# Preparing attention: PE's untaken path as one loop over the halves, five small loads later, the first shift split at once

## The reference

```python
def _L0_attn_ref(x, Wq_d, bq_d, W_qk, b_qk, Wkv_d, bkv_d, Wv_u, bv_u, Wo, bo):   # 32 heads, latent of 4
    C_q = x @ Wq_d + bq_d                                   # (b, s, 12)
    C_kv = x @ Wkv_d + bkv_d                                # (b, s, 4): keys, the same for all heads
    q = (C_q @ W_qk + b_qk).reshape(b, s, NUM_HEADS, KV_LAT)
    scores = jnp.einsum('bqhd,bkd->bhqk', q, C_kv) / jnp.sqrt(jnp.asarray(KV_LAT, x.dtype))
    attn = jax.nn.softmax(scores, axis=-1)
    V = (C_kv @ Wv_u + bv_u).reshape(b, s, NUM_HEADS, HEAD_DIM)
    out = jnp.einsum('bhqk,bkhd->bqhd', attn, V).reshape(b, s, NUM_HEADS * HEAD_DIM)
    return out @ Wo + bo
...
x = x + _L0_attn_ref(_layernorm(x), ...)
x = x + _L0_ffn_ref(_layernorm(x), ...)                     # x @ W.T + bias + sum over 8 LoRA pairs of rank 16
```

## Time and profile before

| | us |
|---|---|
| three runs | 2072.43, 2073.54, 2073.84; median 2073.54 |
| profiled execution | 2071.58 |
| its span | 2069.7 |
| ACT busy, L636 of it | 1968.8, 1900.0 |
| PE busy | 1959.6 |
| DVE, POOL busy | 468.2, 207.3 |

### The profile page before, as it was taken

One profiled execution on the slowest core, in us unless ns is written; L12 is line 12 of the kernel. 1 busy time (PEld: TensorE's weight loads), 2 busy tenths in 40 slices (PEclk: granted clock), 3 DMA queues, 4 the chain that ended last, 5 costly groups with the idle time before them and its releaser, 6 DMA issues.

```text
span 2069.7 us, 36111 instructions
## 1 busy us (share of the span) xinstructions
PE 1959.6 (95%) x15134; PEld 718.4 (35%) x15134; DVE 468.2 (23%) x1134; ACT 1968.8 (95%) x2185; POOL 207.3 (10%) x212
## 2 busy tenths in 40 slices
PE   8878898999999999999999999999999999999999
PEld 5522222333333333333333333333333333333337
DVE  7613433111121210211121111211111111212115
ACT  6699999999999999999999999999999999999980
POOL 5500010000110002000110001100100001100022
PEclk9999999999999999999999999999999999999999
DMA  8532010000010001000010000100010000100011
GB/s 323 149 124 86 3 48 3 5 25 26 13 36 16 18 21 46 5 13 26 26 36 3 26 25 20 30 15 26 15 45 5 25 14 26 36 16 13 25 42 41
DMA packets 45806, 77.43 MB, mean 37 GB/s; under 512 B 15886, under 2 KB 29766, under 8 KB 45642
## 3 DMA queue, kind: packets, MB, share of 16 engines
q1 hardware_dynamic: 43296, 75.02, 10.7%
q10 hardware_dynamic: 2346, 0.09, 0.1%
HBM read 51.23 MB, written 23.86 MB: 36 GB/s over the span
## 4 chain that ended last, share of the span: by engine, by line
ACT 43%; PE 36%; issue 17%; DVE 0%; DVEq 0%
ACT probs L636 43%; PE ps L941 17%; PE ps L986 10%; PE ps L930 6%; PE ps L975 2%; PE ps L964 0%; PE ps L970 0%; PE ps L666 0%; DVE y L1463 0%; PE ps L1083 0%; PE ps L1079 0%; DVE o_t L1519 0%; ACT o_t L651 0%; ACT o_sb L648 0%; DVE recip L1511 0%
## 5 line engine op out<-in xcount | busy, mean ns | idle before, releaser
L636 ACT ACTIVATE probs<-ps 128x1024 f32<-128x1024 f32 x2048 | 1900.0, 1029 | 19.5 <-PE ps L930 8.9
L941 PE MATMUL ps<-probs,c_wide 128*32 128x512 f32 x8192 | 985.2, 598 | 0.0
L930 PE MATMUL ps<-q_in,key_t 27*128 27x512 bf16 x4096 | 404.5, 385 | 97.6 <-ACT probs L636 90.9
L986 PE MATMUL ps<-w_eff,xn_t 128*128 128x512 f32 x1344 | 394.4, 418 | 0.0
L941 PEld LDWEIGHTS ps<-probs,c_wide 128*32 128x32 f32 x8192 | 212.3, 108 | 424.5 <-issue 219.3
L930 PEld LDWEIGHTS ps<-q_in,key_t 27*128 27x128 bf16 x4096 | 103.0, 91 | 726.5 <-ACT probs L636 715.0
L1463 DVE SCALAR_TENSOR_TENSOR y<-ps,nw,y 128x512 f32<-128x512 f32 x64 | 48.1, 751 | 979.4 <-PE ps L986 967.9
L986 PEld LDWEIGHTS ps<-w_eff,xn_t 128*128 128x128 f32 x1344 | 228.1, 188 | 101.9 <-issue 69.8
L536 POOL TENSOR_TENSOR y<-y,ffn_bias 128x1024 f32<-128x1024 f32 x32 | 76.4, 2388 | 1349.0 <-DVEq L1484 1349.0
L531 POOL TENSOR_TENSOR y<-y,attn_bias 128x1024 f32<-128x1024 f32 x32 | 75.8, 2384 | 467.0 <-DMA y<-in_L_attn_x_dram 466.9
L1447 DVE TENSOR_TENSOR y<-ps,y 128x512 f32<-128x512 f32 x56 | 38.7, 692 | 135.4 <-PE ps L964 135.4
(11 more groups left out here) (170 smaller groups left out, 607.0 us busy)
## 6 DMA issues: line engine op xcount, KB each, us to landing
y<-in_L_attn_x_dram SPq DMA_DIRECT2D x40, 512.0 KB, 4.3
out_dram<-y SPq DMA_DIRECT2D x31, 512.0 KB, 2.7
area<-in_L_attn_x_dram SPq DMA_DIRECT2D x16, 512.0 KB, 9.0
q_in<-q_parts SPq DMA_DIRECT2D x256, 27.0 KB
q_parts<-q_parts_sb SPq DMA_DIRECT2D x48, 128.0 KB, 3.0
xn<-in_L_attn_x_dram SPq DMA_DIRECT2D x8, 512.0 KB, 9.1
y<-in_L_attn_Wo_dram SPq DMA_DIRECT2D x1, 2048.0 KB, 8.5
xn<-in_L_attn_Wo_dram SPq DMA_DIRECT2D x1, 2048.0 KB, 13.4
```

The lines of the kernel that those rows point to most:

```text
L636: nc.scalar.activation(probs[:, (c * STEPS + step) % PROBS, bass.ts(pair, 2 * N)], ps[:, 2 * (i % SCORE_SLOTS):2 * (i % SCORE_SLOTS) + 2, ...
L930: last = nc.tensor.matmul(ps[:, at, :], key_t[TILE * h:TILE * h + KEYS, bass.ts(b * KT + kt, P)], q_in[TILE * h:TILE * h + KEYS, g % 2, :] ...
L941: last = nc.tensor.matmul(ps[32 * h:32 * h + 32, SUMS, :], c_wide[:, b * KT + kt, at:at + 32], probs[:, (c * STEPS + step) % PROBS, bass.t ...
L986: last = nc.tensor.matmul(ps[:, SHARED, :], xn_t[:, t % 2, a, kb, :], w_eff[:, b, kb, bass.ts(half, N)], start=(kb + i == 0), stop=(kb == ...
```

## The change

Three edits:

1. In PE's general path the two copies of the loop over chunks, one for each half, become one loop over the halves around one loop over chunks. Since a matmul inside a loop can't choose the half's keys by the loop's variable here, ACT first copies the half's keys and weights into `key_half` and `bound_half`, and PE waits for them (`m_keys`). All of it lies in the path that is jumped over when `tight` is 1.
2. SP's five small loads go from behind `load_tiles(RING + 3)`, ahead of the query stores of chunks 2 to 5, to behind `store_shifts(0, 1, CB)`, ahead of Wv.
3. On DVE the first half's `split_shift` runs through without a break; `scale_parts(7)` and then `split_latents(6)` follow. Before, `split_latents(6)` and `scale_parts(7)` stood between its second and third part.

```diff
@@ sync
             load_tiles(RING + 3)
-            sp.dma_start(bv_rows, ...).then_inc(lora_in, 16)
-            sp.dma_start(coef, ...).then_inc(lora_in, 16)
-            sp.dma_start(attn_bias[:, :], ...).then_inc(lora_in, 16)
-            sp.dma_start(ffn_bias[:, :], ...).then_inc(lora_in, 16)
-            sp.dma_start(lora_a_sb[:, :], ...).then_inc(lora_in, 16)
             for c in range(2, CHUNKS - 4):
                 store_q(c, c % 2)
...
             store_shifts(0, 1, CB)
             sp.wait_ge(t_ready, START + CHUNKS * KB)
             sp.wait_ge(x_measured, CHUNKS)
+            (the same five)
             sp.dma_start(wv_in, wv_u).then_inc(lora_in, 16)
@@ scalar
-                with act.Fori(0, CHUNKS) as c:
-                    nc.scalar.activation(lat[:, 0, :], q_f32[:, bass.ds(c * N, N)], ACT.Abs).then_inc(m_abs, 1)
+                for b in range(B):
+                    nc.scalar.activation(key_half[:, :], key_t[:, b * S:(b + 1) * S], ACT.Copy).then_inc(m_keys, 1)
+                    nc.scalar.activation(bound_half[:, :], bound_w[:, b, :], ACT.Copy).then_inc(m_keys, 1)
+                    with act.Fori(b * CB, (b + 1) * CB) as c:
+                        nc.scalar.activation(lat[:, 0, :], q_f32[:, bass.ds(c * N, N)], ACT.Abs).then_inc(m_abs, 1)
...
@@ tensor
-                for b in range(B):
-                    with pe.Fori(b * CB, (b + 1) * CB) as c:
+                with pe.Fori(0, B) as b:
+                    pe.wait_ge(m_keys, 2)
+                    pe.sem_inc(m_keys, -2)
+                    with pe.Fori(0, CB) as j:
...
-                                                            key_t[TILE * (u // TT):TILE * (u // TT) + KEYS,
-                                                                  b * S + n * N:b * S + (n + 1) * N], start=True, stop=True)
+                                                            key_half[TILE * (u // TT):TILE * (u // TT) + KEYS, bass.ts(n, N)], start=True, stop=True)
...
-                        nc.tensor.matmul(ps[0:H, 6, :], bound_w[:, b, :], lat[:, 0, :], start=True, stop=False).then_inc(m_used, 1)
+                        nc.tensor.matmul(ps[0:H, 6, :], bound_half[:, :], lat[:, 0, :], start=True, stop=False).then_inc(m_used, 1)
...
-                        pe.wait_ge(m_split, c + 1)
+                        pe.wait_ge(m_split, b * CB + j + 1)
@@ vector, split_shift
-                if beside and not then:
-                    beside()
@@ vector, after bounds of the first half
-            split_shift(P, 6, shift_split, bound_max[:, 0:1], None,
-                        lambda: (split_latents(CHUNKS - 2, 0), scale_parts(CHUNKS - 1)))
+            split_shift(P, 6, shift_split, bound_max[:, 0:1])
+            scale_parts(CHUNKS - 1)
+            split_latents(CHUNKS - 2, 0)
```

More of the change, by code:

```diff
@@ L119, in build_block @@
         x_turned = area[:, T + 2 * TT * D:T + 2 * TT * D + KB * N].rearrange("p (k n) -> p k n", k=KB)
+        key_half = nc.alloc_sbuf_tensor_at("key_half", [P, S], BF16, offset=area_at + 4 * (T + TT * D))
+        bound_half = nc.alloc_sbuf_tensor_at("bound_half", [P, H], F32, offset=area_at + 4 * (T + TT * D) + 2 * S)
         key_t = sb("key_t", [P, T], BF16)
@@ L234, in build_block @@
         m_split = sem("m_split")
+        m_keys = sem("m_keys")
         m_read = sem("m_read")
@@ L352, in _ @@
             load_tiles(RING + 3)
[L353 to L358, removed]
             for c in range(2, CHUNKS - 4):
@@ L385, in _ @@
             sp.wait_ge(x_measured, CHUNKS)
+            sp.dma_start(bv_rows, bv_u.rearrange("(g p) -> g p", p=P)).then_inc(lora_in, 16)
+            sp.dma_start(coef, lora_w.rearrange("(n a b) -> n a b", a=1, b=1).to_broadcast([NL, RANK, 1])
+                         ).then_inc(lora_in, 16)
+            sp.dma_start(attn_bias[:, :], bo.rearrange("(a n) -> a n", a=1).to_broadcast([P, D])).then_inc(lora_in, 16)
+            sp.dma_start(ffn_bias[:, :], bias_ffn.rearrange("(a n) -> a n", a=1).to_broadcast([P, D])).then_inc(lora_in, 16)
+            sp.dma_start(lora_a_sb[:, :], lora_a.rearrange("n r d -> (n r) d")).then_inc(lora_in, 16)
             sp.dma_start(wv_in, wv_u).then_inc(lora_in, 16)
@@ L620, in _ @@
             with act.If(act.value_load(tight[:, :], min_val=0, max_val=1) < 1):
-                with act.Fori(0, CHUNKS) as c:
-                    nc.scalar.activation(lat[:, 0, :], q_f32[:, bass.ds(c * N, N)], ACT.Abs).then_inc(m_abs, 1)
-                    act.wait_ge(m_used, 1)
-                    act.sem_inc(m_used, -1)
+                for b in range(B):
[3 more added lines that the diff above has]
+                        nc.scalar.activation(lat[:, 0, :], q_f32[:, bass.ds(c * N, N)], ACT.Abs).then_inc(m_abs, 1)
+                        act.wait_ge(m_used, 1)
+                        act.sem_inc(m_used, -1)
             def exps(c, first):
```

## The result

The changed kernel takes 2066.03 us (median of 7 runs, 2065.57 to 2067.21), the kernel before on the same chip 2073.54 us (7 runs, 2071.23 to 2075.64): a ratio of 0.9967, with the interval 0.9955 to 0.9978, so faster by 7.5 us. The profiled execution after took 2067.13 us, with a span of 2065.3.

What follows compares the result with a forecast made beforehand. PE and ACT, both 95% busy in the attention loop, bound the kernel; the gains lie ahead of it. Profiled 2071.58 - 2.2 - 3.5 - 1.8 = 2064.1; as median 2073.54 - 7.5 = 2066.0 us, range 2064.0 to 2070.4.

Steps and rivals of the forecast that it cites:

- Small loads: First stage, chunk 6: ACT's wait for chunk 2's query store goes, gain 2.2 us, bounds 0 and 2.4.
- R2: Rival: in the first stage another wait replaces the store's, by DVE, POOL or next stores; 2068.2 us, chance 0.13.
- First shift split at once: DVE before the flag `tight`: path to it keeps its distance, cost 0, bounds -0.5 and +0.7 us.
- Jump: PE behind the flag: shorter skip lands in code on hand, gap 4.65 to 1.15 us; gain 3.5, bounds 0 and 3.6.
- R1: Rival: PE's jump keeps its price, or its start hangs on something unseen; 2071.3 us, chance 0.12.
- the rival by proportion: Rival posed for p1: every skipped instruction costs, gap some 3 us, time about 2068 us; no chance given.
- Clock: First attention steps: with the short gap PE's clock does not drop to half; gain 1.8 us, bounds 0 and 1.9.
- R4: Rival: moved small loads hold back `lora_in` and the third group's queries; about 2078 us, chance 0.04 with anything else slower.

Runs made afterwards that it cites:

- b0: The kernel before, unchanged, run again for a second trace: 2073.49 us (10 runs), ratio 1.0.
- a0: The changed kernel, unedited, run again: 2066.51 us (6 runs), ratio 0.9967 against the kernel before.
- u1: The changed kernel with the five small loads back at their old place, ahead of chunk 2's query store: 2069.6 us, ratio 0.9981 against the kernel before.
- o1: The kernel before with only the five small loads moved: 2070.89 us, ratio 0.9989.
- o3: The kernel before with only DVE's new order, the first half's shift split in one piece: 2075.49 us, ratio 1.001.
- n1: The changed kernel with `split_latents(6)` moved off DVE's way to the flag, into later places: 2065.99 us, ratio 0.9968 against the kernel before.
- u3: The changed kernel with DVE's old order around the first half's shift: 2066.33 us, ratio 0.9965 against the kernel before.
- p1: The changed kernel with 36 short matmuls (72 instructions) added to PE's skipped general path: 2066.43 us, ratio 0.997 against the kernel before.
- p2: The changed kernel with 68 short matmuls (136 instructions) added to PE's skipped general path: 2071.05 us, ratio 0.9993 against the kernel before.
- o2: The kernel before with only PE's general path as one loop over the halves: 2068.08 us, ratio 0.9978.
- u2: The changed kernel with PE's general path, and ACT's part of it, back as two copies: 2071.28 us, ratio 0.9989 against the kernel before.
- c1: The changed kernel with PE's general path back as two copies and no filler matmuls between the first attention steps: 2071.52 us, ratio 0.9994 against the kernel before.

## Why the prediction was right

Forecast 2066.0, measured 2066.03. The sum of the traces is best made against b0 (2073.06 us), since it has both the ordinary fourth chunk and the drop of the clock at the end, like the trace of after (2067.13). Up to chunk 6, 61.44 and 61.58: +0.1. Its period, 11.00 and 8.83: -2.2. To the flag, 20.20 and 20.87: +0.7. Gap, 4.82 and 1.43: -3.4. Scores to the seventh exponential, 104.76 - 97.47 = 7.29 and 93.14 + 5.56 - 92.71 = 5.99: -1.3. The rest: +0.1. Together -5.9; the medians give 6.5 (a0 and the runs of the kernel before beside it) to 7.5 (the first runs), within what single executions of one kernel differ.

- *Small loads, -2.2.* Right: -2.0 between the first two traces, -2.2 against b0. That the loads' transfers, 4.3 us by the forecast's estimate, stood ahead of the store was the cause (u1, o1), and R2 fell. The next bound was PE's 8.6 us, as said, within 0.2.
- *First shift split at once, 0 with bounds -0.5 and +0.7.* The step that was wrong, at its upper bound: the way to the flag did not keep its distance, +0.67. "`split_latents` takes their place behind" counted its place and not its company: the 1.93 us of work were in the stretch from 80.4 to 82.5 in which POOL rests, and went to where POOL splits, for 3.7 us. The trace of before had held the answer, on DVE's timeline:
```profile
80.39 0.75 DVE L1250 SCALAR_TENSOR_TENSOR part_f<-part_high,less_high,lat 128x512 f32<-128x512 bf16 x1
...
83.63 1.35 DVE L1205 CAST shift_parts<-shift_f 128x512 bf16<-128x512 f32 x1
85.15 0.84 DVE L1207 TENSOR_TENSOR shift_parts<-shift_f,shift_parts 128x512 bf16<-128x512 f32 x1 [0.17 <-DVEq L1147]
86.65 0.26 DVE L1260 TENSOR_REDUCE c_top<-c_wide 128x4 f32<-128x64 f32 x1 [0.66 <-ACT c_wide L570]
```
What stands at 83.6 is slow, but the two shift operations were short enough that DVE still waited 0.66 us before `c_top`; the three of `split_latents` are not. o3 shows it alone, n1 takes it away. But the old order would not have kept the distance: with the loads moved it costs 0.52 of the 0.67 itself (o1: 20.72; u3: 20.73), by other operations beside POOL. That DVE's work, 2.2 us earlier, would meet POOL's was missing in the term of the loads too.
- *Jump, -3.5.* Right in mechanism and size: -3.2 against the first trace, -3.4 against b0. R1 (the jump keeps its price) and the rival by proportion fell with p1 and p2. The remaining 1.43 us is 0.3 more than SP's 1.15, from which it was taken.
- *Clock, -1.8.* Right for the first trace (7.81 - 5.99 = 1.8 from scores to the seventh exponential), too much for an average one: b0 gives 1.3. The term is not certain either, since the clock also fell in o2 and u3 with the short gap, in the single trace of each. Over all executions the connection holds: with the long gap the mean granted clock is 0.997 to 0.999 in each of 138 executions (of the kernel before, b0, u2, p2, c1, o1 and o3), and with the short gap it is 1.000 in 26 of 51. A mean doesn't say where the clock fell, and the late drop lowers it too; but no execution with the long gap was without a drop, and half of those with the short one were.
- *R4.* Its cover held, with no DMA among PE's waits.

The medians hit the forecast to 0.03 us partly by luck: the loss on the way to the flag was taken as 0, and the medians gain more than the traces. Single executions of the changed kernel also lie near 2065.7 or near 2067.2, by the late drop of the clock; the first median falls in the lower group because four of seven do, and a0's, with three of six, is 2066.51.

## What to carry to other kernels

Code that is never executed has a price where it is jumped over: it was worth more here (4.6 to 5.9 us) than everything that the change moved. The sign of it in a profile is "issue" idle time behind a branch, with a code packet in the middle of it and a second one just behind its end; one packet alone stood in the kernels with the short gap as well. When work changes places or comes earlier on DVE, look up what POOL does at the new place: beside POOL's splits the three operations of `split_latents` took 1.6 to 2.1 times as long here, and the cast in u3 three times. And take a second trace of the kernel before, before trusting a period to half a microsecond.

## What was not expected of the hardware

The jump's price is a step: nothing at 72 more skipped instructions, apart from the 0.64 us that PE stops later on, and 3.5 us at 136 more, with the same code executed.

What the half clock costs behind the gap goes mostly by how much of it falls behind the first scores, and not by the length of the gap. In b0 PE's granted clock is 0.50 from 95.0 to 101.8, with scores at 97.47; in o3 from 98.5 to 105.3, with scores at 98.81:
```profile
95.05:101.80 6.75, 4.33 (x23) 3.13 (x24) 2.81 (x5) 3.18 (x4) 0.00 (x0) 0.50 0.47 59
```
```profile
98.55:105.30 6.75, 6.49 (x36) 3.86 (x40) 0.58 (x1) 4.83 (x6) 0.00 (x0) 0.50 0.85 163
```
Six exponentials take 6.65 us in the first (4.3 us of half clock behind the scores) and 7.59 in the second (6.5 us), against 5.56 at the full clock: 0.25 and 0.31 us lost for each microsecond at 1.2 GHz. The other traces with a drop there give 0.20 (p2 and c1) to 0.30. In u3 the clock fell with a gap of only 1.4 us, for 3.4 us from 94.1 on, and the same six took 99.37 - 92.81 = 6.56. What decides when it falls these runs don't show.
